# A time-ordered recurrence kernel: the division by reciprocal replaced by an exp seed, two squares and four products

## What is computed

```python
# 1: a decayed softmax-like average over time (per batch and channel), k = layernorm(x), v = context
y_t = (e1 * aa + e2 * v_t) / (e1 * bb + e2)      # numerator / denominator
aa, bb = e1b * aa + e2b * v_t, e1b * bb + e2b     # state, decayed by w = -exp(time_decay)
x = x + tanh(g_xattn[0]) * y
# 2: over the batch axis (8 positions) for each time
z = layernorm(x);  h = silu(z_prev * conv0 + z * conv1)
q = silu(h @ Wq); k = h @ Wk; v = h @ Wv; g = h @ Wg          # q, k rotated
# each head's token goes to one of 2 routes by the sign of v . router; q is scaled by score and 1/count
o = tril(q k^T, same route) @ v, normalised over each head
x = x + tanh(g_ffn[0]) * ((silu(g) * o) @ Wout)
```

## Time and profile before

| | |
|---|---|
| median of 3 runs | 2133.79 us (2133.16 to 2134.23) |
| the profiled execution, its own time | 2135.26 us |
| its span | 2133.4 us |
| PE / weight load busy | 1692.9 us (79%) / 820.3 us (38%) |
| DVE busy | 1699.4 us (80%) |
| ACT / POOL busy | 717.8 us (34%) / 764.8 us (36%) |
| mean granted clock of PE | 0.931 |

### The profile page before, as it was taken

One profiled execution on the slowest core, in us unless ns is written; L12 is line 12 of the kernel. 1 busy time (PEld: TensorE's weight loads), 2 busy tenths in 40 slices (PEclk: granted clock), 3 DMA queues, 4 the chain that ended last, 5 costly groups with the idle time before them and its releaser, 6 DMA issues.

```text
span 2133.4 us, 32296 instructions
## 1 busy us (share of the span) xinstructions
PE 1692.9 (79%) x12215; PEld 820.3 (38%) x12215; DVE 1699.4 (80%) x2115; ACT 717.8 (34%) x1252; POOL 764.8 (36%) x772
## 2 busy tenths in 40 slices
PE   0157888888888888888888888888888888888896
PEld 0023443344434443443433444443444444434443
DVE  3887878898788889788878988878898887888852
ACT  4543332333333232333323333332333333323331
POOL 0114323444433344443234444323444432344431
PEclk9988999999999999999999999999999999999998
DMA  9200011001100100110110011011000110100100
GB/s 286 92 10 11 30 31 31 12 20 30 31 30 30 31 12 19 30 31 30 30 31 10 21 30 31 30 30 31 12 19 30 31 30 30 30 16 15 31 11 21
DMA packets 23518, 70.32 MB, mean 33 GB/s; under 512 B 2400, under 2 KB 2656, under 8 KB 23392
## 3 DMA queue, kind: packets, MB, share of 16 engines
q1 hardware_dynamic: 23392, 68.37, 10.7%
HBM read 51.59 MB, written 16.78 MB: 32 GB/s over the span
## 4 chain that ended last, share of the span: by engine, by line
PE 27%; DVE 23%; POOL 21%; issue 20%; ACT 5%; SPq 2%; DMA 1%; POOLq 1%; DVEq 0%; ACTq 0%
PE ps_g L377 7%; PE ps_g L378 7%; PE ps_g L381 7%; DVE fa L922 5%; POOL small L1119 4%; DVE seg L768 3%; POOL small L1111 3%; POOL big L1131 3%; PE ps_s L498 2%; DVE fb L761 2%; PE ps_o L514 2%; POOL big L1148 2%; POOL small L1115 2%; POOL vx L1105 1%; POOL big L1142 1%
## 5 line engine op out<-in xcount | busy, mean ns | idle before, releaser
L377 PE MATMUL ps_g<-big,h_hi 128*128 128x512 f16 x1536 | 616.2, 401 | 59.3 <-issue 36.1
L378 PE MATMUL ps_g<-big,h_hi 128*128 128x512 f16 x1536 | 611.6, 398 | 0.0
L381 PE MATMUL ps_g<-big,h_lo 128*128 128x512 f16 x1536 | 606.9, 395 | 0.0
L1086 POOL TENSOR_TENSOR small<-small 128x1 f32<-128x1 f32 x64 | 14.1, 221 | 921.3 <-DVE small L753 912.5
L377 PEld LDWEIGHTS ps_g<-big,h_hi 128*128 128x128 f16 x1536 | 160.6, 105 | 259.0 <-issue 85.7
L381 PEld LDWEIGHTS ps_g<-big,h_lo 128*128 128x128 f16 x1536 | 157.1, 102 | 202.7 <-issue 37.5
L377 PE MATMUL ps_g<-big 128*128 128x512 f16 x512 | 199.7, 390 | 33.0 <-DVE big L825 33.0
L378 PEld LDWEIGHTS ps_g<-big,h_hi 128*128 128x128 f16 x1536 | 155.9, 102 | 170.5 <-issue 26.8
L922 DVE RECIPROCAL fa<-fa 128x512 f32<-128x512 f32 x64 | 214.1, 3345 | 0.0
L378 PE MATMUL ps_g<-big 128*128 128x512 f16 x512 | 199.7, 390 | 0.0
L381 PE MATMUL ps_g<-big 128*128 128x512 f16 x512 | 198.2, 387 | 0.0
(11 more groups left out here) (143 smaller groups left out, 2849.1 us busy)
## 6 DMA issues: line engine op xcount, KB each, us to landing
x_ring<-in_x SPq DMA_DIRECT2D x32, 512.0 KB
vx<-in_ctx SPq DMA_DIRECT2D x32, 512.0 KB
out<-x_ring SPq DMA_DIRECT2D x32, 512.0 KB
big<-in_wv SPq DMA_DIRECT2D x2, 2048.0 KB, 22.7
big<-in_wg SPq DMA_DIRECT2D x2, 2048.0 KB, 21.9
big<-in_wout SPq DMA_DIRECT2D x2, 2048.0 KB, 16.0
big<-in_wq SPq DMA_DIRECT2D x1, 2048.0 KB, 14.1
big<-in_wk SPq DMA_DIRECT2D x1, 2048.0 KB, 19.5
```

The costliest lines, as they stand in the source:

```text
L377: nc.tensor.matmul(dst[:, :], hi, hi_of(u)[:, kc * HALF:(kc + 1) * HALF], start=(kc == 0), stop=False)
L378: nc.tensor.matmul(dst[:, :], hi, lo_of(u)[:, kc * HALF:(kc + 1) * HALF], start=False, stop=False)
L381: last = nc.tensor.matmul(dst[:, :], lo, hi_of(u)[:, kc * HALF:(kc + 1) * HALF], start=False, stop=(kc == KC - 1))
```

## The change

The quotient is made without a reciprocal. ScalarE reads the bits of the denominator as an integer and takes an Exp of a linear function of it, which gives a seed near 1/denominator in `ek`. VectorE multiplies the denominator and the numerator by the seed (`s_near`, `s_nr`) and forms (d - 2) x n; ScalarE makes ((d - 1)^2 + 0.5)^2 with two Squares; VectorE adds 0.75 and multiplies. The work is in full width, no longer in two halves. On VectorE three operations (`recurrence_ratio`) stand where the division stood, and the fourth (`recurrence_output`) behind the sign, L850. On ScalarE the `seed` stands behind the first copy of v (ahead of L606) and the `polynomial` behind the second (ahead of L621). The Exp of the keys, which writes `ek`, now also waits for the finished quotient. The sign of the quotient is turned, and the gate's Tanh takes scale -1. In the opening, `seed(0)` and `polynomial(0)` stand between `split_unit(0)` and `split_unit(1)` on ScalarE, and the two VectorE parts where the two halves stood.

```diff
+SEED_SLOPE = -LN2 / 2.0 ** 23
+SEED_BIAS = 127.0 * LN2 - 0.0298
...
-            A(tg, tg, ACT.Tanh).then_inc(s_ca, 1)
+            A(tg[:, 0:1], tg[:, 0:1], ACT.Tanh, scale=-1.0).then_inc(s_ca, 1)
+            A(tg[:, 1:2], tg[:, 1:2], ACT.Tanh).then_inc(s_ca, 1)
...
                 after(act, s_ev, j)
+                after(act, s_y, j)
...
+            def seed(n):
+                act.wait_ge(s_den, n + 1)
+                act.wait_ge(s_ekt, 2 * (n + 1))
+                act.wait_ge(s_ev, n + 1)
+                A(ek[:, :], fa[:, :].bitcast(I32), ACT.Exp, scale=SEED_SLOPE, bias=seed_b).then_inc(s_seed, 1)
+            def polynomial(n):
+                act.wait_ge(s_near, n + 1)
+                act.wait_ge(s_nr, n + 1)
+                A(ek[:, :], fa[:, :], ACT.Square, bias=minus_one).then_inc(s_poly, 1)
+                act.wait_ge(s_poly, 2 * n + 1)
+                A(ek[:, :], ek[:, :], ACT.Square, bias=half_c).then_inc(s_poly, 1)
...
                     copy_v(i, 0)
                     if opening(i):
                         split_unit(5)
+                if nxt:
+                    seed(n)
+                if main:
                     act.wait_ge(s_qtp, i + 1)
...
+                if nxt:
+                    polynomial(n)
+                if main:
                     act.wait_ge(s_dl, 2 * (i + 1))
...
             split_unit(0)
+            act.wait_ge(s_seed_c, 3)
+            seed(0)
+            polynomial(0)
             split_unit(1)
...
                 if nxt:
-                    recurrence_output(n, 0)
-                if nxt:
-                    recurrence_output(n, 1)
+                    recurrence_ratio(n)
...
                     V.tensor_scalar(sgn, sgn, -1.0, None, ALU.add).then_inc(s_sgn, 1)
+                if nxt:
+                    recurrence_output(n)
...
-                V.reciprocal(fa[:, part], fa[:, part]).then_inc(s_rec, 1)
+                dve.wait_ge(s_seed, n + 1)
                 dve.wait_ge(s_num, n + 1)
-                dve.wait_ge(s_rec, 2 * n + g + 1)
-                V.tensor_tensor(fb[:, part], fb[:, part], fa[:, part], ALU.mult).then_inc(s_y, 1)
+                V.tensor_tensor(fa[:, :], fa[:, :], ek[:, :], ALU.mult).then_inc(s_near, 1)
+                V.tensor_tensor(fb[:, :], fb[:, :], ek[:, :], ALU.mult).then_inc(s_nr, 1)
+                dve.wait_ge(s_near, n + 1)
+                dve.wait_ge(s_nr, n + 1)
+                V.scalar_tensor_tensor(fb[:, :], fa[:, :], 2.0, fb[:, :], ALU.subtract, ALU.mult).then_inc(s_cor, 1)
+            def recurrence_output(n):
+                dve.wait_ge(s_cor, n + 1)
+                dve.wait_ge(s_poly, 2 * (n + 1))
+                V.scalar_tensor_tensor(fb[:, :], ek[:, :], 0.75, fb[:, :], ALU.add, ALU.mult).then_inc(s_y, 1)
```

More of the change, by code:

```diff
@@ L34 @@
 F32 = mybir.dt.float32
+I32 = mybir.dt.int32
 F16 = mybir.dt.float16
@@ L65 @@
 H_TOP = 2.0 ** 15
+LN2 = 0.6931471805599453
+SEED_SLOPE = -LN2 / 2.0 ** 23
+SEED_BIAS = 127.0 * LN2 - 0.0298
 G_TOP = 2.0 ** 14
@@ L145, in flamingo_layer @@
         head_m = sb("head_m", [P, HG])
-        small = sb("small", [P, 370])
+        small = sb("small", [P, 373])
         at = [0]
@@ L183, in flamingo_layer @@
         usc = col(2)
+        seed_b, minus_one, half_c = col(1), col(1), col(1)
         carry_b = sb("carry_b", [P, CB * BB])
@@ L208, in flamingo_layer @@
         s_sca, s_scb, s_sva, s_svb = sem("scan_den"), sem("scan_num"), sem("save_den"), sem("save_num")
-        s_den, s_num, s_rec, s_y, s_x2 = (sem(n) for n in
-            ("den_done", "num_done", "recip_done", "y_done", "x2_done"))
+        s_den, s_num, s_y, s_x2 = (sem(n) for n in ("den_done", "num_done", "y_done", "x2_done"))
+        s_seed_c = sem("seed_consts")
+        s_seed, s_near, s_nr, s_cor, s_poly = (sem(n) for n in
+            ("den_seeded", "den_near_one", "num_seeded", "num_corrected", "poly_done"))
         s_bn2, s_ag2, s_rs2, s_nb2, s_xn = (sem(n) for n in
@@ L916, in numerator, with recurrence_ratio @@
                 add_state(fb[:, :], s_num)
-            def recurrence_output(n, g):
-                part = slice(g * HALF, (g + 1) * HALF)
-                dve.wait_ge(s_den, n + 1)
-                V.reciprocal(fa[:, part], fa[:, part]).then_inc(s_rec, 1)
+            def recurrence_ratio(n):
+                dve.wait_ge(s_seed, n + 1)
                 dve.wait_ge(s_num, n + 1)
-                dve.wait_ge(s_rec, 2 * n + g + 1)
-                V.tensor_tensor(fb[:, part], fb[:, part], fa[:, part], ALU.mult).then_inc(s_y, 1)
+                V.tensor_tensor(fa[:, :], fa[:, :], ek[:, :], ALU.mult).then_inc(s_near, 1)
[7 more added lines that the diff above has]
+                V.scalar_tensor_tensor(fb[:, :], ek[:, :], 0.75, fb[:, :], ALU.add, ALU.mult).then_inc(s_y, 1)
             def output_transpose(n):
-                dve.wait_ge(s_y, 2 * (n + 1))
+                dve.wait_ge(s_y, n + 1)
                 V.transpose(fa[:, :], fb[:, :]).then_inc(s_yt, 1)
@@ L1028, in _ @@
             V.memset(decay[:, :], 0.0).then_inc(s_cv, 1)
+            for cols, value in ((seed_b, SEED_BIAS), (minus_one, -1.0), (half_c, 0.5)):
+                V.memset(cols, value).then_inc(s_seed_c, 1)
             V.memset(ones, 1.0).then_inc(s_cv, 1)
@@ L1033, in _ @@
             dve.wait_ge(s_cv, 10)
-            dve.wait_ge(s_ca, 6)
+            dve.wait_ge(s_ca, 7)
             V.tensor_copy(cbt(decay[:, :])[:, :, :, 1:SEG],
@@ L1053, in _ @@
             spread(3, 2)
-            recurrence_output(0, 0)
+            recurrence_ratio(0)
             set_scale(2)
@@ L1057, in _ @@
             lo_unit(0)
-            recurrence_output(0, 1)
+            recurrence_output(0)
             set_scale(3)
```

## The result

The changed kernel takes 2065.6 us (median of 4 executions, 2060.2 to 2073.2) against 2133.5; the ratio is 0.9684, 95% interval 0.9653 to 0.9715. That is 68 us less where 36 were forecast.

What follows compares the result with a forecast made beforehand. No engine is full; hand-overs from VectorE through POOL's norm and route to PE bound a step. 30 us from the steps and 6 from the opening gave 2099.3 us (2098 from the median), range 2068 to 2120.

Steps and rivals of the forecast that it cites:

- The path and the cap: At L863, PE's sign sums L473 let only 1.3 us pass in 23 steps, nothing in 7: 30 us, bounds 20 and 30.
- the cover: VectorE's wait at L863 for the sign sums: up to 1.7 us more VectorE work there would cost nothing.
- VectorE's saving: Per looped step, the 7.97 us division goes and four operations of 5.00 us come: 2.97 us saved.
- the estimate by that rule, 2.0 us: By the skill's port rule, the first product waits out POOL's L1142, about 1 us: saving 2.0 us, not 3.0.
- ScalarE: Seed, two squares and two extra table loads a step fit into waits; all costed at nothing, seed with 11 us of cover.
- The opening: Recurrences 0 and 1, division on VectorE's own path, each give up to 3.0 us: 6 us, bounds 0 and 6.
- TensorE's clock: Low clock behind PE's pause before L479; a shorter pause of 2.5 us need not save it; costed at nothing.
- the sum: Profiled execution: 2135.3 - 30 - 6 = 2099.3 us; from the median 2133.8 - 36 = 2098.
- the rival's 23 x 0.9 = 21 us: Clock comes back: less idling, fewer slow steps before L479 or in the output projections; 21 us more, 2077; chance 0.17.
- The stated range: The forecast's own was 2088 to 2110 us; with rivals and room for a mix, 2068 to 2120.

Runs made afterwards that it cites:

- the 0.6 us: The changed kernel with one more VectorE operation of 128x512 behind the transpose of y, ahead of L896: 2067.2 us, ratio 0.9681.
- the 2.5 us: The changed kernel with two more VectorE operations of 128x1024 behind the transpose of y, ahead of L896: 2122.9 us, ratio 0.9950.
- The kernel without any of it: The kernel before with the second half's reciprocal left out, without seed, squares or added table loads: 2061.7 us, ratio 0.9682.
- The filled kernel before: The kernel before with 12 more f16 products of 128x512 in PE's pause ahead of L479, division untouched: 2080.2 us, ratio 0.9753.
- the early copy: The kernel before with the copy of the carried denominator (L758) moved to the end of the step before: 2107.1 us, ratio 0.9866.
- one filler: The changed kernel with 10 filler products in PE's pause ahead of L486 and the carry's copy moved early: 2024.1 us, ratio 0.9484.
- with both: The changed kernel with 10 products ahead of L486, 5 ahead of the output projections, and the carry's copy moved early: 2018.7 us.

## Why the prediction was right or wrong

**The path and the cap: right.** L896 starts at 39.2 us of an ordinary step where L863 started at 40.5, the 1.3 us forecast, and it waits for the sign sums in every looped step. The stretch gave 37 us instead of 30, since only 3 steps and not 7 had a low head; with 7 it would have been 30. That part is not the forecast's doing: a low head costs 1.6 us in the changed kernel, its count lies between 0 and 8 in the kernels here, and what sets it is not shown. More VectorE time in the cover is free (the 0.6 us), and taking VectorE's saving back takes back the gain (the 2.5 us).

**VectorE's saving: 2.3 us, not 2.97.** In most steps the first product met POOL's L1184 and took 2.13 us where the second took 1.21. The Trainium skill (SBUF — State Buffer, "Who interferes with whom") says that a VectorE instruction with two SBUF inputs contends with a GpSimd instruction that reads SBUF. The trace agrees, and the estimate by that rule, 2.0 us, was the closer one. It did not matter: 0.96 us of waiting were left to cover it, not 1.7.

**ScalarE: right.** Passes of 1.15 us, loads of 1.28, the seed 9.7 us ahead of its reader in the step shown and at least 4.9 in any. The kernel without any of it took the same time. The squares had only 0.4 us to spare before L965, as worked out. The drain of about 1380 ns that the Trainium skill (ScalarE: Activation LUTs, "What ACT_TABLE_LOAD costs") adds to a load did not show: 1.30 us from the load's start to its activation in 84 of 124 cases. The Silu of the gate (L708), said to wait for PE still, did so less often (17 waits, 33 before), since its load now fills that time.

**The opening: right.** 6.5 us for 6 (8.5 in the second execution).

**TensorE's clock: the step that failed.** The prediction saw a low clock behind a pause of 2.93 us as well as behind one of 3.77, concluded that "a shorter pause of 2.5 us need not save the clock", and cost the clock "at nothing in the sum". The mechanism stood among the rivals with a chance of 0.17 and 21 us. It was worth more: 26 us from L969 to L958, and 7 through the heads. The filled kernel before shows it by itself: 53 us with VectorE untouched. With the pause filled in both kernels no step has a low stretch behind it, and then the change is worth 35 us, with the forecast's 36 inside the spread of 26 to 45. So the mechanism of the sum was right and one term, set at zero, was about 26 to 33 us.

Two readings led there. The first is the step with the pause of 2.93 us. Its projections ahead of the pause had begun at the low clock too, and in all ten steps of that kind, 7 before and 3 after, the stretch from L969 to L958 took 6.3 us or more; of the other 27 steps with a pause of 2.92 us in the changed kernel 14 had no low stretch at all. I read one step of each kind and took the worse one for the rule. The second is the ordinary step. Its 1.9 us at 0.53, from 1043.2 on, are only the end of the low stretch, which began with L479 itself, here in the kernel before:

```profile
1041.60:1045.00 3.40, 3.38 (x22) 1.43 (x23) 1.12 (x2) 2.72 (x9) 0.00 (x0) 0.50 0.45 108
```

So an ordinary step lost up to 1.7 us there, not 0.9. That the rival's 23 x 0.9 = 21 us lies near the measured 26 is luck: its price was about half of what a step loses, and about half of the steps came free.

**The rest of the gain** is the head of the step with what follows it, 5 us, not foreseen; it comes from the collision of the carry's copy, which the late load of x moves in some steps. In the second execution of the same kernel it is 1 us. Against it stand 7 us more between L958 and the next step: the first norm waits 79.5 us in all for the load of x, where it waited 46.2 before.

**The stated range.** By its own bounds, 20 to 30 us in the steps and 0 to 6 in the opening, the forecast's own range is 2098 to 2114, not the stated 2088 to 2110.

## What to carry to other kernels

Where PE waits in every step, write down each stretch at the low clock as a term of its own, with both its values, before setting it to zero: here an earlier release of 1.3 us was worth 2.1 a step. Independent products put into such a pause cost nothing while they end before the awaited operand comes (12 did in the kernel before; 5 ahead of the output projections made PE 0.3 us late), and they tell in one run how much the clock holds. And before a wait is moved out of the way, ask what the waiting operation's own time was hidden behind.

## What the runs showed of the hardware that was not expected

- 384 products more, into a bank that nobody reads then, made the kernel 53 us faster (2080 against 2133 us), with the mean granted clock 0.965 in place of 0.931.
- The changed kernel's executions spread over 0.6 and 0.7% in its two measurements (2050.7 to 2073.2 us over both), and their granted clocks go with it (0.949 to 0.940); the kernel before had 0.15%. With the early copy the spread is 0.16% with one filler (2022.0 to 2025.2) and 0.17% with both (2016.4 to 2019.9).
- Behind one and the same pause of PE, 2.92 us, the granted clock stayed high in 14 of 30 steps and was low for a part of what followed in 16.
- A VectorE copy of 128x64 takes 0.2 us alone and 2.0 us beside a POOL product of 128x1024 that started just before it. Moved away it shifts the cost: POOL's next product takes 3.28 instead of 2.36 us.
